# A graph kernel's relational passes: TensorE turns tile i-1 first, sums tile i, makes the first sums of tile i+1, and transforms tile i-1 last

## The chip, the cores and the metric

The kernel runs on one core of one Trainium2 chip. The metric is the device time of one execution in microseconds (us); lower is better. Ahead of the change three runs gave a median of 5129.6 us, from 5125.4 to 5138.4.

## What is computed

There are 6250 nodes with 256 features and 106,250 edges sorted by destination, each with one of 8 types. Two layers are computed: a relational one of three inner passes, and one of attention.

```python
h = relu(layernorm(x))
for l in range(3):                        # the relational layer
    xr  = einsum('nd,rde->rne', h, W_rel[l])              # 8 tables of every node
    agg = segment_sum(xr[edge_type, src], dst)            # a row of a table per edge
    h   = relu(agg + h @ W_root[l] + bias[l])
x = x + h
h = relu(layernorm(x)) @ Wv + bv          # the attention layer
attn = softmax over the edges of each destination of leaky_relu(q[src] + k[dst])
out = x + segment_sum(h[src] * attn, dst)
```

## The kernel before

All is float32. The nodes stand in NT = 49 tiles of 128, the edges that are no self-loops in 787 chunks of up to 128, and four chunks are a group (197 groups). The self-loop of a node needs no gather: its row of the table is on the chip when the tile is transformed.

The program has five stages: the first transform of every tile (to about 377 us), pass 0, pass 1 and pass 2 of the relational layer (`l` = 0, 1, 2), and the attention. A pass begins with the table of transformed rows in DRAM (8 x 256 values per node) and does this:

- **Gathers.** GpSimd (POOL) issues one indirect DMA per chunk (L676, `gather_pass`), which fetches 128 rows of 1 KB into a slot of `ring`. The ring holds RINGS = 10 groups. For group n POOL waits until the window sums of group n - 10 are done (semaphore `quad_done`).
- **Window sums** (the first step, L1755, `sum_windows`). The destinations of a chunk lie in a window of 32 nodes, so TensorE (PE) multiplies a mask of 128 x 32 with the chunk into 32 rows of `pair_ps`, and counts `quad_done` up once per group. Two groups are a pair. ScalarE (ACT) copies each pair out of `pair_ps` (L1503, `keep_pairs`) into one of four places. `pair_ps` has two halves, so the sums of pair p wait for the copy of pair p - 2. A tile needs about two new pairs; `new_pairs` gives them in two halves, early and late.
- **Tile sum** (L1769, `sum_tile`): seven matmuls over the kept pairs into `both_sums`. In pass 0 two more ahead of them add the root term (L1766). VectorE (DVE) adds `root` and writes `z` (L1235, `sum_up`).
- **Turn and transform** (L1646 and L1661). PE transposes z into `turn_ps`, ACT applies relu and writes `xT` (L1447), and PE multiplies xT with the next weights: four banks of 512 columns, and last the root part in a fifth bank, which lies beside `turn_ps`. ACT copies three banks into `stage` (L1509), DVE the fourth (L916). DVE adds the eight self-loop terms into `root` (L941, each waits for the one before), and last the fifth bank (L926). SyncE stores the tile of the next table.

In passes 0 and 1 PE's order in step i is: early window sums of tile i, turn of tile i-1, late window sums of tile i, transform of tile i-1, tile sum of tile i. ACT's is: early pair, relu of tile i-1, late pair, banks of tile i-1. Each engine runs its instructions in the order in which they are written and waits on semaphores; no scheduler comes between. In pass 0 DVE also adds eight self-loop terms of this pass for each tile, out of rows loaded from the table (L951, `add_first_loops`). In pass 2 the small product `to_h` (L1798) stands in the place of the transform, and a normalisation on DVE and ACT lies between the tile sum and the turn.

## Time and profile before

| what | value |
|---|---|
| median of 3 runs | 5129.6 us |
| the profiled execution | 5129.3 us, its span 5127.6 us |
| busy: PE, DVE, ACT, POOL | 3293.8, 1890.7, 1236.4, 3151.2 us |
| mean granted TensorE clock | 0.774 of full speed |
| pass 0, pass 1, pass 2, first to last gather | 1148.1, 1129.7, 1122.8 us |
| between last gather and next pass's first | 55.6, 52.9, 40.4 us |
| attention, from its first gather to the end | 1200.8 us |

The three passes with what follows each of them take 3549.5 us, 69% of the span. "Gather" stands for the instruction on POOL that issues one. A matmul in float32 has two records in the trace, so the seven of a tile sum are shown as x14. A matmul's record has the start from the profiler and an end that is modelled; when its result was signalled is seen only at those who wait for it. A row of the windows view gives a stretch, its length, then for PE, its weight loads, DVE, ACT and POOL the busy time with the count of instructions, then the granted TensorE clock, the share of busy DMA engines and GB/s. A row of a timeline ends with the idle time of its engine just before and what ended it, in brackets; rows of other engines and weight loads are left out. The releaser "remote" is one that the profile could not name.

### The profile page before, as it was taken

How to read it: one execution, taken by the hardware profiler on the slowest of the kernel's cores; microseconds unless marked ns; L12 is line 12 of the kernel's file. 1: busy time of each engine (PE TensorE's matmuls, PEld its weight loads, DVE VectorE, ACT ScalarE, POOL GpSimd, SP SyncE). 2: the span in 40 equal slices, each digit the busy share in tenths (PEclk: the TensorE clock that was granted, in tenths of full speed). 3: DMA queues.
4: the chain of work that ended last, by engine and by line, in shares of the span. 5: the costliest groups of instructions: out<-in, count | busy, mean ns of one | idle time of the engine just before them, and what ended most of it. 6: DMA issues, size and time to landing. Idle time of an engine off the chain costs nothing.

```text
span 5127.6 us, 48875 instructions
## 1 busy us (share of the span) xinstructions
PE 3293.8 (64%) x14171; PEld 1990.6 (39%) x14171; DVE 1890.7 (37%) x4736; ACT 1236.4 (24%) x2949; POOL 3151.2 (61%) x3305
## 2 busy tenths in 40 slices
PE   9994777776773676777665434443344677676666
PEld 4442333333431333333332223222222555565555
DVE  4543444443542232332232122222223454544444
ACT  2220111111110111111111000000002666666665
POOL 1126666666665666666664667676764666666664
PEclk9995888878886787888787666666666878778888
DMA  6544555554653344444443333333332333333332
GB/s 210 187 183 132 190 185 191 185 186 167 204 182 129 122 144 130 141 135 139 133 142 104 99 102 106 104 103 101 106 101 77 102 103 102 101 103 102 100 100 79
DMA packets 239997, 680.99 MB, mean 133 GB/s; under 512 B 60188, under 2 KB 111988, under 8 KB 215028
## 3 DMA queue, kind: packets, MB, share of 16 engines
q0 software_dynamic: 152400, 419.03, 28.0%
q1 hardware_dynamic: 73256, 245.85, 13.0%
q10 hardware_dynamic: 14076, 12.93, 0.9%
q8 instruction: 124, 2.03, 0.2%
q14 instruction: 141, 1.16, 0.1%
HBM read 501.99 MB, written 175.58 MB: 132 GB/s over the span
## 4 chain that ended last, share of the span: by engine, by line
another core or an unknown queue 31%; PE 29%; issue 14%; POOL 12%; DVE 6%; DMA 6%; ACT 2%; DVEq 1%; POOLq 0%; ACTq 0%; SPq 0%
PE bank L1661 18%; POOL ring L676 12%; DMA ring<-h_table,code 5%; PE pair_ps L1755 4%; PE both_sums L1769 4%; DVE root L941 2%; PE turn_root L1646 1%; ACT stage L1509 1%; PE bank L1798 0%; ACT xT L1447 0%; PE turn_root L1661 0%; DVE z L1235 0%; DVEq L940 0%; DVE z L907 0%
## 5 line engine op out<-in xcount | busy, mean ns | idle before, releaser
L676 POOL DMA_INDIRECT ring<-table,code x2361 | 2327.0, 986 | 1225.8 <-issue 733.7
L1661 PE MATMUL bank<-wide,xT 128*128 128x512 f32 x2352 | 1181.9, 660 | 206.9 <-ACT xT L1447 145.9
L676 POOL DMA_INDIRECT ring<-h_table,code x787 | 747.9, 950 | 461.4 <-issue 249.8
L1661 PEld LDWEIGHTS bank<-wide,xT 128*128 128x128 f32 x2352 | 489.1, 215 | 850.6 <-issue 660.7
L1769 PE MATMUL both_sums<-masks 128*128 128x256 f32 x2058 | 550.4, 426 | 320.2 <-issue 174.7
L1503 ACT COPY masks<-pair_ps 128x512 f32<-128x512 f32 x297 | 173.2, 583 | 2143.0 <-remote 1480.6
L1769 PEld LDWEIGHTS both_sums<-masks 128*128 128x128 f32 x2058 | 445.6, 219 | 416.7 <-issue 341.6
L1866 PE MATMUL pair_ps<-ring,stage 128*128 x1764 | 519.6, 445 | 98.1 <-ACT stage L1583 97.2
L1755 PE MATMUL pair_ps<-ring,masks 128*32 128x256 f32 x4722 | 450.3, 478 | 127.5 <-DMA ring<-table,code 76.6
L1646 PE MATMUL turn_root<-ident,z 128*128 128x128 f32 x392 | 104.1, 356 | 564.3 <-DVE z L1235 247.9
L1866 PEld LDWEIGHTS pair_ps<-ring,stage 128*128 128x128 f32 x1764 | 380.9, 229 | 159.1 <-issue 104.7
L941 DVE SCALAR_TENSOR_TENSOR root<-bank,loops,root 128x256 f32<-128x256 f32 x686 | 330.7, 482 | 197.1 <-ACT stage L1509 83.9
L1373 DVE TENSOR_SCALAR masks<-masks,ring 128x128 f32<-128x128 f32 x882 | 199.1, 303 | 487.4 <-issue 273.3
L1646 PEld LDWEIGHTS turn_root<-ident,z 128*128 128x128 f32 x392 | 49.6, 166 | 663.1 <-DVE z L1235 282.0
L1816 PE MATMUL bank<-ident,masks 128*128 128x128 f32 x931 | 174.3, 317 | 188.3 <-issue 117.2
L1261 DVE TENSOR_TENSOR stage<-both_sums,root 128x256 f32<-128x256 f32 x49 | 20.8, 425 | 722.3 <-remote 416.9
L1509 ACT COPY stage<-bank 128x512 f32<-128x512 f32 x294 | 170.4, 588 | 465.8 <-PE bank L1661 346.3
L1567 ACT ACTIVATE masks<-node_row,local 128x128 f32<-128x128 f32 x931 | 281.8, 393 | 0.0
L1755 PEld LDWEIGHTS pair_ps<-ring,masks 128*32 128x32 f32 x4722 | 151.3, 126 | 331.6 <-issue 277.3
L1235 DVE TENSOR_TENSOR z<-both_sums,root 128x256 f32<-128x256 f32 x98 | 41.5, 424 | 621.3 <-remote 482.8
L1544 ACT ACTIVATE wide<-bank,low_key 128x512 f32<-128x512 f32 (+1 forms) x245 | 163.6, 668 | 413.6 <-PE bank L1816 201.3
L1822 PE MATMUL bank<-ident,wide 128*128 128x128 f32 x931 | 182.0, 328 | 98.7 <-ACT wide L1577 84.8
(247 smaller groups left out, 2841.2 us busy)
## 6 DMA issues: line engine op xcount, KB each, us to landing
table<-stage SPq DMA_DIRECT2D x144, 1024.0 KB
back<-table SPq DMA_DIRECT2D x49, 1024.0 KB
ring<-table,code POOLq DMA_INDIRECT x2361
ring<-h_table,code POOLq DMA_INDIRECT x787
h_table<-stage SPq DMA_DIRECT2D x49, 130.0 KB
back<-h_table ACTq DMA_DIRECT2D x49, 130.0 KB
features<-xT SPq DMA_DIRECT2D x49, 128.0 KB, 4.0
first_T<-features SPq DMA_DIRECT2D x49, 128.0 KB
```

Of the source, the lines that this page charges most:

```text
L676: pool.indirect_dma_start(slot(c % RING, width), None, table, bass.IndirectOffsetOnAxis(ap=code[:, c:c + 1], axis=0)).then_inc(landed[n % ...
L941: nc.vector.scalar_tensor_tensor(root[:, i, :], bank[t // 2][:, t % 2 * D:(t % 2 + 1) * D], loop_weight(i, t), root[:, i, :] if t else bia ...
L1373: last = nc.vector.tensor_scalar(masks[:, b, s, :], masks[:, b, s, :], -FAR, source, ALU.mult, ALU.add)
L1509: nc.scalar.copy(stage[:, b, 512 * q:512 * (q + 1)], bank[q][:, :]).then_inc(evacuated[q], 1)
L1567: last = nc.scalar.activation(masks[:, b, s, :], node_row[:, :], ACT.Abs, scale=-1.0, bias=local[:, bass.ds(i, 1), s])
L1646: last = nc.tensor.transpose(turn_ps[:, k, :], z[:, b, k * P:(k + 1) * P], ident[:, :])
L1661: last = nc.tensor.matmul(bank[q][:, 0:width], xT[:, b, k, :], weights[:, k, 512 * q:512 * q + width], start=(k == 0), stop=(k == K - 1))
L1755: last = nc.tensor.matmul(pair_ps[p % 2][at_row:at_row + WINDOW, q % PAIR * D:(q % PAIR + 1) * D], window_masks(k)[:, c % CHUNKS_AT_ONCE, ...
L1769: last = nc.tensor.matmul(sum_ps[b][:, 0:D], masks[:, b, s, :], quad_sums(first_quad(i) + s), start=(s == 0 and l > 0), stop=(s == SPAN - 1))
L1816: last = nc.tensor.transpose(score_ps[c % 2][:, s % GROUP * P:(s % GROUP + 1) * P], masks[:, b, s, :], ident[:, :])
L1822: last = nc.tensor.transpose(attn_ps[c % 2][:, s % GROUP * P:(s % GROUP + 1) * P], scores[b][:, s * P:(s + 1) * P], ident[:, :])
L1866: last = nc.tensor.matmul(pair_ps[b][:, 0:D], attn_slot(s), at_offset(where[0][s]) if s < SLOTS else own_rows[:, b, 0:D], start=(s == 0), ...
```

## The change

The order of the three passes is another; no arithmetic is added or removed. On PE step i becomes: turn of tile i-1, tile sum of tile i, all window sums of tile i+1, transform of tile i-1 with its root part first. The window sums of tile 0 stand ahead of the loop. PE now waits, ahead of the turn, until DVE has added the root part of the tile before. On ACT relu comes first, then the pairs of tile i+1, then the banks. On DVE the tile before is evacuated (`next_table(l, i - 1, ...)`), its root part is added first and takes over the addition of the bias, and the self-loop terms follow. POOL's code and its waits are unchanged. SyncE's code is unchanged as well.

```diff
@@ -92,9 +92,7 @@
         return max(t for t in range(NT) if first_quad(t) // PAIR <= p) + 1
 
     def new_pairs(t):
-        pairs = range(pairs_to(t - 1), pairs_to(t))
-        half = (len(pairs) + 1) // 2
-        return pairs[:half], pairs[half:]
+        return range(pairs_to(t - 1), pairs_to(t))
 
...
@@ -910,8 +908,11 @@
             def evacuate(l, i, use, b, first=False, bias_at=False):
                 q = R // 2 - 1
                 if not first:
+                    dve.wait_ge(transformed[b], CREDIT + NB * use + 1)
+                    nc.vector.tensor_tensor(root[:, i, :], bank[NB - 1][:, 0:D], bias_row[:, :], ALU.add
+                                            ).then_inc(evacuated[NB - 1], 1)
                     add_loops(l, i, use, b, range(0, R - 2))
-                dve.wait_ge(transformed[b], CREDIT + NB * use + q + 1)
+                dve.wait_ge(transformed[b], CREDIT + NB * use + (q + 1 if first else q + 2))
                 dve.wait_ge(stored[b], table_stored(l, b, use))
                 nc.vector.tensor_copy(stage[:, b, 512 * q:512 * (q + 1)], bank[q][:, :]).then_inc(evacuated[q], 1)
                 if first:
@@ -920,11 +921,6 @@
                     nc.vector.tensor_copy(root[:, i, :], bias_row[:, :]).then_inc(evacuated[NB - 1], 1)
                     return
                 add_loops(l, i, use, b, range(R - 2, R))
-                dve.wait_ge(transformed[b], CREDIT + NB * use + NB)
-                settle(dve, loops_done((l - 1) * NT + i, R))
-                dve.wait_ge(root_step, loops_done((l - 1) * NT + i, R))
-                nc.vector.tensor_tensor(root[:, i, :], bank[NB - 1][:, 0:D], root[:, i, :], ALU.add
-                                        ).then_inc(evacuated[NB - 1], 1)
 
             def loop_weight(i, t):
                 return loops[:, bass.ds(i, 1), t]
@@ -935,11 +931,13 @@
                     if t % 2 == 0 and t // 2 < R // 2 - 1:
                         settle(dve, CREDIT + l * NT + i + 1)
                         dve.wait_ge(evacuated[t // 2], CREDIT + l * NT + i + 1)
-                    if t:
+                    if t == 0:
+                        dve.wait_ge(evacuated[NB - 1], CREDIT + l * NT + i + 1)
+                    else:
                         settle(dve, loops_done((l - 1) * NT + i, t))
                         dve.wait_ge(root_step, loops_done((l - 1) * NT + i, t))
                     nc.vector.scalar_tensor_tensor(root[:, i, :], bank[t // 2][:, t % 2 * D:(t % 2 + 1) * D], loop_weight(i, t),
-                                                   root[:, i, :] if t else bias_row[:, :], ALU.mult, ALU.add
+                                                   root[:, i, :], ALU.mult, ALU.add
...
@@ -1250,7 +1250,9 @@
                     upcoming_masks(l, i + 2)
                     if l == 0 and i + 1 < NT:
                         add_first_loops(i + 1, (i + 1) // 2, 1 - b)
-                    next_table(l, i, j, b)
+                    if i:
+                        next_table(l, i - 1, (i - 1) // 2, 1 - b)
+                next_table(l, NT - 1, PAIRS, 0)
...
@@ -1516,28 +1518,28 @@
 
             for l in range(L - 1):
                 conv_head(l)
+                keep_pairs(l, new_pairs(0))
                 for i in range(NT + 1):
-                    early, late = new_pairs(i) if i < NT else ((), ())
-                    keep_pairs(l, early)
                     if i:
                         j, b = divmod(i - 1, 2)
                         use = (l + 1) * USES[b] + j
                         relu_turned(use, b, transformed[b], NB * use)
-                    keep_pairs(l, late)
+                    if i + 1 < NT:
+                        keep_pairs(l, new_pairs(i + 1))
                     if i:
                         for q in range(R // 2 - 1):
                             keep_bank(l + 1, use, b, q)
 
             conv_head(L - 1)
+            keep_pairs(L - 1, new_pairs(0))
             for i in range(NT + 1):
-                early, late = new_pairs(i) if i < NT else ((), ())
-                if i:
-                    deviation(NT + i - 1)
-                keep_pairs(L - 1, early)
                 if i:
                     j, b = divmod(i - 1, 2)
                     relu_turned(L * USES[b] + j, b, h_ready[b], j)
-                keep_pairs(L - 1, late)
+                if i < NT:
+                    deviation(NT + i)
+                if i + 1 < NT:
+                    keep_pairs(L - 1, new_pairs(i + 1))
...
@@ -1776,17 +1778,18 @@
             for l in range(L - 1):
                 far_conv(l)
                 pe.wait_ge(weights_loaded, weights_of(l + 1))
+                sum_windows(l, new_pairs(0))
                 for i in range(NT + 1):
-                    early, late = new_pairs(i) if i < NT else ((), ())
-                    sum_windows(l, early)
                     if i:
                         j, b = divmod(i - 1, 2)
+                        pe.wait_ge(evacuated[NB - 1], CREDIT + (l + 1) * NT + i - 1)
                         turn_sum(l, j, b)
-                    sum_windows(l, late)
-                    if i:
-                        transform((l + 1) * NT + i - 1, (l + 1) * USES[b] + j, b, AHEAD + REST)
                     if i < NT:
                         sum_tile(l, i, i // 2, i % 2)
+                    if i + 1 < NT:
+                        sum_windows(l, new_pairs(i + 1))
+                    if i:
+                        transform((l + 1) * NT + i - 1, (l + 1) * USES[b] + j, b, ROOT_FIRST)
...
+            sum_windows(L - 1, new_pairs(0))
             for i in range(NT + 1):
-                early, late = new_pairs(i) if i < NT else ((), ())
-                sum_windows(L - 1, early)
                 if i:
                     j, b = divmod(i - 1, 2)
                     turn(L * USES[b] + j, b)
-                sum_windows(L - 1, late)
+                if i < NT:
+                    sum_tile(L - 1, i, i // 2, i % 2)
+                if i + 1 < NT:
+                    sum_windows(L - 1, new_pairs(i + 1))
                 if i:
                     to_h(j, b)
```

On PE, in the middle of pass 1 (line numbers of each program's own text), this stands before for one step and the first row of the next:

```order
L1755 MATMUL pair_ps<-ring,masks 32x256 x8
L1646 MATMUL turn_root<-ident,z 128x128 x2
L1755 MATMUL pair_ps<-ring,masks 32x256 x8
L1661 MATMUL bank<-wide,xT 128x512 x8
L1661 MATMUL turn_root<-wide,xT 128x256 x2
L1769 MATMUL both_sums<-masks 128x256 x7
```

And this now:

```order
L1648 MATMUL turn_root<-ident,z 128x128 x2
L1771 MATMUL both_sums<-masks 128x256 x7
L1757 MATMUL pair_ps<-ring,masks 32x256 x16
L1663 MATMUL turn_root<-wide,xT 128x256 x2
L1663 MATMUL bank<-wide,xT 128x512 x8
```

The two halves of the window sums are joined and stand between the tile sum and the transform; the turn no longer stands between them.

On ACT, at the same place, one step before:

```order
L1503 COPY masks<-pair_ps 128x512
L1447 ACTIVATE xT<-turn_root 128x256
L1503 COPY masks<-pair_ps 128x512
L1509 COPY stage<-bank 128x512 x3
L1503 COPY masks<-pair_ps 128x512
```

And now, one step and the first rows of the next:

```order
L1449 ACTIVATE xT<-turn_root 128x256
L1505 COPY masks<-pair_ps 128x512 x2
L1511 COPY stage<-bank 128x512 x3
L1449 ACTIVATE xT<-turn_root 128x256
L1505 COPY masks<-pair_ps 128x512 x2
```

The relu (ACTIVATE) no longer stands behind a pair copy of its own step; the bank copies still stand behind two.

On DVE, one tile of pass 0 before:

```order
L1235 TENSOR_TENSOR z<-both_sums,root 128x256
L971 SCALAR_TENSOR_TENSOR masks<-row_node,node_row 128x896
L962 TENSOR_TENSOR masks<-rel_T,node_row 128x512
L951 SCALAR_TENSOR_TENSOR root<-back,loops,root 128x256 x8
L941 SCALAR_TENSOR_TENSOR root<-bank,loops,bias_row 128x256
L941 SCALAR_TENSOR_TENSOR root<-bank,loops,root 128x256 x5
L916 COPY stage<-bank 128x512
L941 SCALAR_TENSOR_TENSOR root<-bank,loops,root 128x256 x2
L926 TENSOR_TENSOR root<-turn_root,root 128x256
```

And now:

```order
L1235 TENSOR_TENSOR z<-both_sums,root 128x256
L969 SCALAR_TENSOR_TENSOR masks<-row_node,node_row 128x896
L960 TENSOR_TENSOR masks<-rel_T,node_row 128x512
L949 SCALAR_TENSOR_TENSOR root<-back,loops,root 128x256 x8
L912 TENSOR_TENSOR root<-turn_root,bias_row 128x256
L939 SCALAR_TENSOR_TENSOR root<-bank,loops,root 128x256 x6
L917 COPY stage<-bank 128x512
L939 SCALAR_TENSOR_TENSOR root<-bank,loops,root 128x256 x2
```

The addition of the root bank moved from the end of the tile's additions to their head, but stands behind the masks and the eight additions of `add_first_loops`. From `L912` on the rows belong to tile i-1, where before all rows belonged to tile i.

## Rows read from the trace of the kernel before

**Rows 1.** Windows of three passes and one end: stretch, its us, then by engine.

```profile
377.30:1525.40 1148.10, 799.79 (x3424) 436.91 (x3425) 513.90 (x1066) 146.54 (x274) 780.21 (x787) 0.80 0.54 182
1581.00:2710.70 1129.70, 743.21 (x3133) 380.57 (x3134) 314.25 (x588) 146.34 (x274) 769.89 (x787) 0.78 0.42 135
2710.70:2763.60 52.90, 48.40 (x206) 26.27 (x205) 25.23 (x51) 11.09 (x21) 0.00 (x0) 1.00 0.25 97
2763.60:3886.40 1122.80, 451.36 (x2411) 275.78 (x2412) 237.78 (x715) 82.58 (x184) 776.89 (x787) 0.63 0.35 103
```

**Rows 2.** What the gathers of pass 0 waited for: us, times.

```profile
  PE pair_ps L1755: 74.8, 23
  remote: 67.2, 26
```

**Rows 3.** The same for pass 1 and, last two, pass 2.

```profile
  remote: 98.6, 34
  PE pair_ps L1755: 36.5, 15
...
  remote: 95.9, 30
  PE pair_ps L1755: 22.3, 9
```

**Rows 4.** Timeline, one step in pass 1: start, us, engine, line.

```profile
2272.54 1.37 POOL L676 DMA_INDIRECT ring<-table,code  x1 [2.28 <-PE pair_ps L1755]
...
2273.33 10.09 PE L1661 MATMUL bank<-wide,xT 128*128 128x512 f32 x16 [1.85 <-ACT xT L1447]
2274.22 0.94 POOL L676 DMA_INDIRECT ring<-table,code  x1 [0.30 <-issue]
...
2284.12 3.19 PE L1769 MATMUL both_sums<-masks 128*128 128x256 f32 x14
...
2287.23 1.07 PE L1755 MATMUL pair_ps<-ring,masks 128*32 128x256 f32 x16
...
2291.36 0.44 PE L1646 MATMUL turn_root<-ident,z 128*128 128x128 f32 x2 [3.06 <-DVE z L1235]
...
2295.20 0.59 ACT L1503 COPY masks<-pair_ps 128x512 f32<-128x512 f32 x1 [12.88 <-PE pair_ps L1755]
```

**Rows 5.** Timeline of PE, then of ACT, at the start of pass 1.

```profile
1623.50 1.08 PE L1755 MATMUL pair_ps<-ring,masks 128*32 128x256 f32 x8 [3.90 <-DMA ring<-table,code]
...
1639.30 0.59 ACT L1503 COPY masks<-pair_ps 128x512 f32<-128x512 f32 x1 [33.72 <-remote]
1675.70 0.59 ACT L1503 COPY masks<-pair_ps 128x512 f32<-128x512 f32 x1 [35.81 <-remote]
```

**Rows 6.** Timeline of POOL: first gathers after three pauses.

```profile
2249.64 1.37 POOL L676 DMA_INDIRECT ring<-table,code  x1 [1.96 <-remote]
...
3311.34 0.94 POOL L676 DMA_INDIRECT ring<-table,code  x1 [4.83 <-remote]
...
2852.22 0.95 POOL L676 DMA_INDIRECT ring<-table,code  x1 [7.64 <-remote]
```

**Rows 7.** Windows from the gather after one pause to the next pause's end.

```profile
2238.00:2249.60 11.60, 7.77 (x56) 4.91 (x54) 6.38 (x13) 2.00 (x5) 7.55 (x8) 0.96 0.55 182
...
3265.50:3311.30 45.80, 18.95 (x104) 11.73 (x104) 10.48 (x33) 3.59 (x8) 31.54 (x32) 0.65 0.36 103
...
2763.60:2852.20 88.60, 8.65 (x64) 1.85 (x64) 2.67 (x3) 1.76 (x3) 61.74 (x64) 0.50 0.34 101
```

**Rows 8.** Groups by line, 400 to 1600 us: two that pass 0 alone has.

```profile
L951 DVE SCALAR_TENSOR_TENSOR root<-back,loops,root 128x256 f32<-128x256 f32 x392 | 190.8, 487 | 12.3
...
L1766 PE MATMUL both_sums<-first_root,first_T 128*128 128x256 f32 x196 | 51.3, 385 | 3.3 <-issue 3.3
```

**Rows 9.** Timeline, a step in the end of pass 1.

```profile
2740.12 7.13 PE L1661 MATMUL bank<-wide,xT 128*128 128x512 f32 x16 [0.47 <-ACT xT L1447]
...
2747.09 1.03 PE L1661 MATMUL turn_root<-wide,xT 128*128 128x256 f32 x4
```

12 lines of the change are left out of this document (6 added, 6 removed).

## Prediction

> **What bounds the kernel now.** First the windows view, by stage [rows 1]. In pass 0 and in pass 1 all 787 gathers are issued while PE is busy 799.8 and 743.2 us; in pass 2, which has no transform, PE is busy 451.4 us only. Yet the three take 1148.1, 1129.7 and 1122.8 us. The reader is to see that PE's work fell by 292 us from pass 1 to pass 2 and the pass by 7 us. So PE's throughput is not the bound, and an order that merely packs PE better is worth little while gathers run. Behind the last gather it is another matter: in the 52.9 us after pass 1 PE is busy 48.4 us [rows 1].
>
> Then POOL. One gather takes 0.94 us, with 0.30 us before it [rows 4], a pace of 1.24 us, and 787 of them 976 us. Pass 1 is 154 us above that. POOL's waits on window sums are 98.6 + 36.5 = 135.1 us in 49 pieces, those of pass 0 74.8 + 67.2 = 142.0 us in 49, those of pass 2 95.9 + 22.3 = 118.2 us in 39 [rows 2, 3]. The pauses are the difference between a pass and its floor.
>
> Then what a pause waits for. In the timeline POOL waits 2.28 us until 2272.54. The transform starts at 2273.33, the tile sum at 2284.12, the window sums at 2287.23, the turn at 2291.36, and ACT's next copy of a pair only at 2295.20, after 12.88 us without work [rows 4]. The window sums take 1.07 us, but their signal is seen 8 us after their start. The start of pass 1 shows the same with nothing else on PE: its eight groups of window sums have all started by 1623.50, and ACT can copy the third pair at 1639.30 and the fourth at 1675.70 [rows 5]. The signals of PE behind window sums come late while gathers run back to back, and in one burst when POOL pauses. I can't name the mechanism from the trace, but its price can be read off. After 8 gathers the pause is 1.96 us, after 32 it is 4.83, after 64 it is 7.64 [rows 6, 7]. A line through the first and the last is 1.15 + 0.101 x n us for n gathers; at 32 it gives 4.4. At n = 16, which is 787/49, it gives 2.8 us, and 135.1/49 is 2.76. So the part of 0.101 us per gather, 80 us in a pass, is paid however the work is cut. Only the constant goes away with fewer pauses: 1.15 - 0.30 (the idle time of a common gather) = 0.85 us each.
>
> **The change, part by part.** *What is added and removed.* Per tile the DVE addition of the root bank, the eight of the self-loops and all matmuls stay in number. One wait of PE for the root addition is new; queued behind it stand the turn, the tile sum and the window sums, and for these waits ACT. I cost it at nothing in passes 1 and 2: the addition now is the first of its tile, and PE has the rest of a transform (7.13 us in the full clock) to run over it [rows 9]. POOL's and SyncE's queues are passed by nothing.
>
> *The relu ahead of the pair copies.* Before, ACT's relu stands behind an early pair copy, so the transform starts only after a burst [rows 4]. Now xT is made before the window sums are issued. What is late next is the tile sum of i+1, which needs pairs copied after the burst. From burst to next window sums there were 14.7 us (2272.54 to 2287.23), of which the transform took 10.1 [rows 4]; and the late half stood behind the turn, at 2291.7. If the transform has run ahead of the burst, turn, tile sum and window sums follow within some 5 us (0.4 + 3.2 + copies 1.2).
>
> *What that gives POOL.* A burst of one tile's window sums lets it issue 16 gathers, 20 us. If a further tile's signals get through before these are over, the pause comes after 32 gathers. Pass 2 has just this short PE step, and 787/39 = 20 gathers per pause on average, with stretches of 32 [rows 3, 7]. The new order issues window sums earlier than pass 2 does, as they no longer stand behind a turn that waits for z. I take 28 pauses in each pass (one per 28 gathers), between 49 (nothing gained) and 12 (one per 64, the longest in the rows). Sum: (49 - 28) x 0.85 = 18 us in pass 0 and in pass 1, (39 - 28) x 0.85 = 9 us in pass 2; 45 us together.
>
> *The end of a pass.* The window sums now run one tile ahead of the transform. When the last gather has landed, one transform more is left in passes 0 and 1: 7.1 + 0.9 = 8.0 us [rows 9], 16 us in two. Against that, of a step of about 12.4 us in the end (transform 8, tile sum 3.2, turn 0.4) some 1 us was the wait for z and relu, which is now covered; over four steps that is 4 us, 8 us in two passes. The net is +8 us; bounds 0 (the transform has run ahead) and +16. In pass 2 it is one small product and I leave it out.
>
> *Pass 0's DVE.* The root addition stands behind the masks and behind eight additions of 0.49 us, 3.9 us together [rows 8]. The turn waits for it. It is hidden if POOL's 20 us are not used up, else see the rival.
>
> *The clock.* PE's granted clock is 0.80 and 0.78 in passes 0 and 1, a mix of its two levels, and 1.00 in the end of pass 1 [rows 1]. The transform takes 7.13 us at full clock [rows 9] and 10.09 us after an idle stretch [rows 4]. If it directly follows the window sums it may run faster, but a faster PE has no buyer here, as pass 2 shows. I cost it at nothing.
>
> **A rule that says otherwise.** The trace has a window sum's signal up to some 50 us late [rows 5]. The Trainium skill, page "TensorE: Matmul & The Clock Gate", section "The cost: per-tile semaphore tail", gives the time from matmul to signal for tiled matmuls as 25 + 4.7 per tile + 26.3 per increment, in ns; for four tiles and one increment that is about 70 ns, an estimate from this page. By that rule nothing but the chain of PE, ACT and DVE would hold the ring, the new order would cut that chain, and the pauses would go. This trace doesn't agree. As a mechanism of this kernel it is the last rival below.
>
> **The sum.** The profiled execution took 5129.3 us (span 5127.6), as good as the median of 5129.6. 5129.3 - 45 + 8 = 5092 us.
>
> **Rivals.**
> - *The pauses keep their number.* Signals that are dispatched after a burst still come with the next. For it: at the start of pass 1 signals issued on a free PE came 16 and 50 us late [rows 5], and pass 1 has a pause per 16 gathers like clockwork. Against it: pass 2's 39. Time: 5129 + 8 = 5137 us.
> - *Slower: the transform is held too.* If PE can't run its transform until the window sums are signalled, each step after a burst is transform, turn, tile sum and window sums in series: the 14.7 us of rows 4, the turn's 0.4 and 1.1 for the second half of the window sums, 16.2 us. That is within POOL's 20 us. In pass 0 the 3.9 us of DVE come in, if the turn waits for the root addition in full, and the two additional matmuls ahead of its tile sum; their four records of 0.385 us overlap like those of the tile sum (3.19 us for 14, so 0.23 each), 0.9 us [rows 4, 8]. That is 21.0 us, 1.0 us too long, 49 times. It decides from 3.8 us of additional delay upward. Time: 5129 + 49 + 8 = 5186 us.
> - *Long stretches.* Window sums get so far ahead that POOL pauses once per 64 gathers. 37 pauses fewer in passes 0 and 1 (31 us each), 27 in pass 2 (23 us): 5129 - 86 + 8 = 5051 us. The only stretch of that length stands at a pass's start.
> - *Signals in time, no pauses.* 142 + 135 + 118 us of waits less the 137 x 0.30 that stay: 5129 - 354 = 4775 us. Rows 5 speak against it.
>
> **How the numbers follow.** The forecast has a chance of 0.50 (5075 to 5114), unchanged pauses 0.21, slower 0.18, long stretches 0.08, no pauses 0.03. The range of 5045 to 5150 holds the first, the second and the fourth, and the beginning of the third. Three tenths of a per cent, 15 us, are about what a measurement can tell from no change. Faster: the forecast nearly whole, the long stretches and the last, 0.59. Same: the second, 0.22. Slower 0.19.
>
> **What would show it.** In the profile after: the windows of the passes near 1130, 1112 and 1114 us; POOL's waits on window sums in about 28 pieces per pass instead of 49; between a burst and the next window sums some 5 us instead of 14.7; transform rows that start right behind window sums and not behind ACT's xT; and 55 us rather than 52.9 behind pass 1's last gather. I am wrong if the pauses stay at 49, or if the time falls although their number stays: then the law of 1.15 + 0.101 n is no property of the gathers but one of the order. I am wrong the other way if POOL's pauses become longer than the line allows for their stretch, which would show a ring that PE's serial step holds.

## The result and the profile after

On one chip, with the kernels run in turn, the kernel before took 5128.19 us (median of 12, 5123.12 to 5147.35) and the changed one 5144.26 us (median of 12, 5134.15 to 5150.48). The ratio is 1.0023, interval 1.0013 to 1.0034: 16 us slower, where 37 us less than 5129 were forecast. That is inside the 0.3% within which the prediction speaks of no change, though the interval leaves out 1. The time lies in the range given, but the gain that was forecast isn't there. The profiled execution took 5149.1 us (span 5147.3), against 5129.3 before.

The windows view of the changed kernel, for passes 0, 1 and 2, each followed by the stretch between its last gather and the next first one (columns as in [rows 1]):

```profile
376.20:1526.00 1149.80, 848.47 (x3404) 463.16 (x3405) 508.73 (x1056) 146.98 (x271) 779.56 (x787) 0.82 0.54 179
1526.00:1597.80 71.80, 60.89 (x235) 34.14 (x233) 42.33 (x85) 13.05 (x24) 0.00 (x0) 0.95 0.36 134
1597.80:2731.90 1134.10, 782.82 (x3142) 402.19 (x3142) 306.52 (x578) 146.92 (x271) 766.36 (x787) 0.80 0.42 134
2731.90:2791.00 59.10, 53.51 (x196) 28.85 (x196) 30.42 (x61) 12.95 (x24) 0.00 (x0) 0.99 0.23 95
2791.00:3910.70 1119.70, 499.43 (x2452) 283.79 (x2452) 243.07 (x723) 81.95 (x185) 772.24 (x787) 0.66 0.36 103
3910.70:3944.20 33.50, 19.73 (x102) 13.82 (x102) 15.83 (x61) 11.90 (x33) 0.00 (x0) 0.81 0.12 33
```

Against [rows 1] and the table of the profile before, the passes are +1.7, +4.4 and -3.1 us, their ends +16.2, +6.2 and -6.9 us, and the attention +2.3. So the passes hardly moved and the ends cost 15.5 us. (One profile of each kernel stands behind these differences.)

The gathers' waits by releaser, in pass 0, pass 1 and pass 2 of the changed kernel (us, times; they answer to [rows 2, 3]):

```profile
  remote: 86.0, 38
  PE pair_ps L1757: 58.1, 12
...
  remote: 99.7, 42
  PE pair_ps L1757: 43.3, 12
...
  remote: 96.3, 26
  PE pair_ps L1757: 20.9, 5
```

That is 50, 54 and 31 pauses with 144.1, 143.0 and 117.2 us, where there were 49, 49 and 39 with 142.0, 135.1 and 118.2. The forecast was 28 in each. In passes 0 and 1 there is still one pause for each of the 49 tiles. Pass 2 did lose eight of its 39, and the pass got 3.1 us shorter, but its waits fell by 1.0 us only, where the prediction's law (1.15 us for each pause) takes 9.2 away. What got shorter is POOL's busy time, 772.24 us against 776.89, so the fewer pauses gave nothing that these profiles show.

The timeline shows why the number stayed. One step of pass 1 of the changed kernel:

```profile
2580.55 9.25 PE L1663 MATMUL bank<-wide,xT 128*128 128x512 f32 x16
...
2580.93 0.94 POOL L674 DMA_INDIRECT ring<-table,code  x1 [2.34 <-remote]
...
2589.85 3.19 PE L1771 MATMUL both_sums<-masks 128*128 128x256 f32 x14
...
2592.97 1.81 PE L1757 MATMUL pair_ps<-ring,masks 128*32 128x256 f32 x23
...
2602.11 2.04 PE L1757 MATMUL pair_ps<-ring,masks 128*32 128x256 f32 x3 [0.76 <-issue]
2603.52 0.42 DVE L1235 TENSOR_TENSOR z<-both_sums,root 128x256 f32<-128x256 f32 x1 [12.02 <-remote]
2603.70 0.59 ACT L1505 COPY masks<-pair_ps 128x512 f32<-128x512 f32 x1 [13.27 <-remote]
2603.85 0.95 POOL L674 DMA_INDIRECT ring<-table,code  x1 [3.19 <-remote]
...
2604.07 0.80 PE L1663 MATMUL turn_root<-wide,xT 128*128 128x256 f32 x1
```

The burst, in which the signals that had been held back are seen together while POOL stands still, is at 2580.9; the next window sums start at 2593.0, 12.0 us later, not 5. Between them stand nearly the whole transform (four banks, 9.25 us) and the tile sum (3.19 us). The transform didn't run ahead of the burst: PE's order puts it behind all window sums of the tile to come. One step on, the last of these were issued at 2602.1, and the transform starts at 2604.07, after the next burst. Nothing that the tile sum or the window sums signalled in between was seen: DVE had been idle for 12.02 us when it took up a tile sum that had started at 2589.85, and ACT for 13.27 us when it took up a pair, both while POOL stood still. In this step, then, one burst admits one tile, as before.

### The profile page after: what moved, and what is told of

It reads as the page before. It is cut to its first block, busy times and chain, and to the rows that moved or that the text cites. A ratio compares the mean times of both kernels' runs of the same rounds, so it can differ in the third digit from the quotient of the medians.

```text
span 5147.3 us, 49020 instructions
## 1 busy us (share of the span) xinstructions
PE 3435.7 (67%) x14171; PEld 2048.1 (40%) x14171; DVE 1889.3 (37%) x4736; ACT 1238.2 (24%) x2949; POOL 3144.4 (61%) x3305
## 3 DMA queue, kind: packets, MB, share of 16 engines
q14 instruction: 140, 1.15, 0.1%
## 4 chain that ended last, share of the span: by engine, by line
PE 36%; issue 21%; another core or an unknown queue 17%; POOL 12%; DMA 7%; DVE 4%; DVEq 1%; ACT 1%; SPq 0%; POOLq 0%; ACTq 0%
PE bank L1663 16%; POOL ring L674 12%; PE both_sums L1771 7%; PE pair_ps L1757 7%; DMA ring<-h_table,code 6%; PE turn_root L1663 2%; DVEq L1234 1%; PE turn_root L1648 1%; DMA back<-table 1%; DVE root L949 1%; PE both_sums L1768 1%; PE bank L1801 1%; DVE root L939 1%; DVE masks L969 0%
## 5 line engine op out<-in xcount | busy, mean ns | idle before, releaser
L1663 PE MATMUL bank<-wide,xT 128*128 128x512 f32 x2352 | 1138.0, 632 | 60.0 <-issue 56.1
L1757 PE MATMUL pair_ps<-ring,masks 128*32 128x256 f32 x4722 | 555.9, 409 | 497.4 <-issue 407.6
L1771 PE MATMUL both_sums<-masks 128*128 128x256 f32 x2058 | 588.4, 448 | 342.6 <-issue 243.6
L1663 PEld LDWEIGHTS bank<-wide,xT 128*128 128x128 f32 x2352 | 477.0, 206 | 639.3 <-issue 629.1
L1771 PEld LDWEIGHTS both_sums<-masks 128*128 128x128 f32 x2058 | 469.4, 233 | 438.6 <-issue 354.5
L1757 PEld LDWEIGHTS pair_ps<-ring,masks 128*32 128x32 f32 x4722 | 193.1, 112 | 801.5 <-issue 720.9
L939 DVE SCALAR_TENSOR_TENSOR root<-bank,loops,root 128x256 f32<-128x256 f32 x784 | 378.2, 482 | 283.7 <-ACT stage L1511 159.7
L960 DVE TENSOR_TENSOR masks<-rel_T,node_row 128x512 f32<-128x512 f32 (+1 forms) x150 | 101.5, 679 | 381.2 <-remote 341.5
L1648 PE MATMUL turn_root<-ident,z 128*128 128x128 f32 x392 | 90.2, 312 | 221.7 <-DVE root L912 114.4
L1819 PEld LDWEIGHTS bank<-ident,masks 128*128 128x128 f32 x931 | 128.3, 163 | 251.8 <-issue 238.5
```

The lines of the kernel that those rows point to most:

```text
L939: nc.vector.scalar_tensor_tensor(root[:, i, :], bank[t // 2][:, t % 2 * D:(t % 2 + 1) * D], loop_weight(i, t), root[:, i, :], ALU.mult, AL ...
L1663: last = nc.tensor.matmul(bank[q][:, 0:width], xT[:, b, k, :], weights[:, k, 512 * q:512 * q + width], start=(k == 0), stop=(k == K - 1))
L1757: last = nc.tensor.matmul(pair_ps[p % 2][at_row:at_row + WINDOW, q % PAIR * D:(q % PAIR + 1) * D], window_masks(k)[:, c % CHUNKS_AT_ONCE, ...
L1771: last = nc.tensor.matmul(sum_ps[b][:, 0:D], masks[:, b, s, :], quad_sums(first_quad(i) + s), start=(s == 0 and l > 0), stop=(s == SPAN - 1))
L1819: last = nc.tensor.transpose(score_ps[c % 2][:, s % GROUP * P:(s % GROUP + 1) * P], masks[:, b, s, :], ident[:, :])
```

## The experiments

All times below are medians beside the kernel before on the same chip. These runs were made on four chips (numbers 11, 0, 7 and 2; the number of the first result's chip isn't on record, and "the first chip" below is the one of that result). On all four the kernel before takes 4714 to 4716 us, and in the profiles POOL doesn't pause in the passes at all, unless an edit makes it wait. So they can't show the pauses; they show the rest in the clear, which is the word for it below.

"End 0" is the stretch from pass 0's last gather to pass 1's first, "end 1" and "end 2" are those after the next two passes.

The theory: the new order has no hold on the pauses, since the transform still stands behind the window sums' waits, and the loss is made behind the last gathers, by one transform more and by SyncE's store ahead of the load. The rivals: the order does bring window sums earlier, and something else eats the gain; or the loss comes from the pauses.

**1. SyncE stores one tile later.** The changed kernel with

```diff
-                    elif i > 1:
-                        store_next(l + 1, i - 2, b)
+                    elif i > 2:
+                        store_next(l + 1, i - 3, 1 - b)
                 if l < L - 1:
+                    store_next(l + 1, NT - 3, 0)
                     store_next(l + 1, NT - 2, 1)
```

> The changed kernel, but in passes 0 and 1 SyncE issues the store of tile i-3 where it issued that of tile i-2, so that the loads for tile i+1 no longer stand behind a store whose data come one step later than before. Theory A (the end of pass 0 grew by 16 us, of which 8 to 9 us are one transform more and the rest is DVE waiting 1.5 to 2.4 us per step for rows loaded behind that store): the stretch from pass 0's last gather to pass 1's first falls from 71.8 to some 63 us, the passes themselves stay at 1150, 1134, 1120 us, total some 5136 us. Rival B (the load is late for its own length, not for the queue): 5144 us, stretch 72 us.

Measured: 4728.18 us against 4716.25, ratio 1.0024 (1.0015 to 1.0033). The expected times were written for the first chip and are some 400 us off in this run and the next three; only differences count. End 0 is 48.1 us, and 12 us of the loss are still there. What the store takes from it is seen beside run 5.

**2. Transform ahead of the window sums.** The changed kernel with both orders turned round in passes 0 and 1, on PE (below) and likewise ACT's bank copies ahead of its pair copies:

```diff
-                    if i + 1 < NT:
-                        sum_windows(l, new_pairs(i + 1))
                     if i:
                         transform((l + 1) * NT + i - 1, (l + 1) * USES[b] + j, b, ROOT_FIRST)
+                    if i + 1 < NT:
+                        sum_windows(l, new_pairs(i + 1))
```

> The changed kernel, but in passes 0 and 1 the transform of tile i-1 stands ahead of the window sums of tile i+1 on PE, and the bank copies ahead of the pair copies on ACT. Theory A (the number of POOL's pauses and their length don't depend on PE's order, and the end of a pass pays for the transform that lags by one tile more): passes within 6 us of 1150, 1134 and 1120 us, the two ends fall by 8 us each to some 60 and 52 us with four transforms behind the last gather, total some 5125 us. Rival B (the transform was run in the shade of the window sums and now delays them by 8 us per step): pauses get longer, passes 0 and 1 above 1160 us, total above 5170 us.

Measured: 4716.85 us against 4716.25, ratio 1.0003 (0.9994 to 1.0012): no loss. The rival's slower passes aren't there either: 1011.4, 1006.4 and 1006.5 us.

**3. The new order in pass 2 alone.** The kernel before, with PE's and ACT's order of the change in pass 2 only:

```diff
-                sum_windows(L - 1, early)
...
-                sum_windows(L - 1, late)
-                if i:
-                    to_h(j, b)
                 if i < NT:
                     sum_tile(L - 1, i, i // 2, i % 2)
+                if i + 1 < NT:
+                    sum_windows(L - 1, all_pairs(i + 1))
+                if i:
+                    to_h(j, b)
```

> The kernel before, with the new order in pass 2 alone. Theory A (the parts add up: pass 2 gained 3 us and its end 7 us, everything lost lies in passes 0 and 1): 5118 us, pass 2 at 1120 and its end at 33.5 us. Rival B (the differences of pass 2 are those between two executions): 5128 us.

Measured: 4717.19 us against 4716.25, ratio 0.9999 (0.9990 to 1.0008). Pass 2's part of the change does nothing to the time that can be measured here. Its windows serve as those of the old order in passes 0 and 1; the three ends:

```profile
1389.60:1433.00 43.40, 36.23 (x114) 19.57 (x114) 20.86 (x43) 7.00 (x13) 0.00 (x1) 0.91 0.21 84
2438.90:2475.80 36.90, 32.41 (x98) 17.16 (x96) 16.75 (x35) 6.42 (x12) 0.04 (x1) 0.96 0.23 90
3482.30:3508.30 26.00, 14.55 (x56) 10.23 (x54) 11.06 (x45) 9.24 (x27) 0.04 (x2) 0.76 0.11 33
```

**4. Window sums that don't read the ring.** The kernel before; the window sums still wait for the landing but read the weights' tile, so that the sums hold other numbers:

```diff
-window_masks(k)[:, c % CHUNKS_AT_ONCE, :], slot(c % RING, D),
+window_masks(k)[:, c % CHUNKS_AT_ONCE, :], wide[:, 0:D],
```

> The kernel before, with window sums that multiply a fixed piece of the weights in SBUF with the masks, not the rows gathered into the ring; all waits and signals stay (so the sums are of other numbers). Theory C (TensorE's reading of the ring, into which transfers write, is what makes the window sums come late): the sums come at once, POOL pauses seldom, each pass falls towards 1010 to 1060 us, total 4790 to 4950 us. Rival D (it is not the place that is read: waits, signals or the gathers' own backlog): pauses as before, 5128 us.

Measured: 4715.18 us against 4716.25, ratio 0.9996 (0.9987 to 1.0005). It was to tell the cause of the pauses, and there were none; it says only that reading the ring costs nothing measurable here.

**5. The changed kernel again.** Unchanged.

> The changed kernel, unchanged, timed once more beside the kernel before. On the chip of the first result it took 5144.3 us against 5128.2, and POOL paused about 50 times in passes 0 and 1 in both kernels. On the chip of the four runs so far POOL does not pause in the passes at all and the kernel before takes 4716.3 us. Theory: the loss is made behind the last gathers and has nothing to do with the pauses, so it stays in us whatever the pace is: the ends of passes 0, 1 and 2 take 16 and 6 us more and 7 us less, in sum 10 to 16 us slower (4726 to 4732 us where the kernel before takes 4716), with end 0 at 58 to 62 us against 43. The kernel that differs from this one only in that SyncE stores tile i-3 lost 12 us with an end 0 of 48.0, so if the loss were in SyncE's order alone this kernel would lose 12 + 10. Rival: the loss comes from the pauses or from the slower pace; then this kernel is within 0.1 per cent of the kernel before wherever there are no pauses.

Measured: 4731.24 us against 4715.26, ratio 1.0038 (1.0024 to 1.0051): 16 us slower, as on the first chip, with no pause in its profile. Its windows, as above:

```profile
377.40:1394.10 1016.70, 763.23 (x3502) 441.38 (x3502) 523.65 (x1080) 153.29 (x278) 777.17 (x787) 0.86 0.62 205
1394.10:1446.10 52.00, 44.46 (x136) 23.95 (x136) 29.99 (x61) 9.13 (x17) 0.00 (x0) 0.93 0.33 130
1446.10:2451.20 1005.10, 722.54 (x3220) 386.76 (x3221) 315.63 (x594) 153.96 (x279) 765.66 (x787) 0.81 0.48 153
2451.20:2495.30 44.10, 39.68 (x120) 21.32 (x118) 22.05 (x45) 8.54 (x16) 0.04 (x2) 0.96 0.25 99
2495.30:3500.90 1005.60, 475.22 (x2500) 280.16 (x2501) 247.48 (x739) 88.71 (x191) 766.19 (x787) 0.66 0.40 115
3500.90:3526.90 26.00, 14.59 (x56) 10.27 (x54) 11.06 (x45) 9.22 (x27) 0.04 (x2) 0.76 0.12 33
```

Passes 1 and 2 go at POOL's pace, 787 gathers in 1005 us, with PE busy 722.5 us in one and 475.2 in the other. The ends are 52.0, 44.1 and 26.0 against 43.4, 36.9 and 26.0 in run 3: 8.6 + 7.2 = 15.8 us, about the loss of 16.0. This sum is good to a few us only: end 2 takes 24.6 us with the old order, as in run 9's second kernel; end 0 with the old order lies between 39.5 and 43.4 us in the profiles of runs 3, 4 and 9; and the execution profiled here took 4737.8 us, 6.6 above its median.

Much of the spread of end 0 lies ahead of PE's work, in the landings of the last gathers. From the last window sums that wait for a landing (1395.98 here) to pass 1's first gather (1446.12) there are 50.1 us; with the old order the same stretch is 41.1 us in run 3, 40.7 in run 4 and 40.7 in run 9's second kernel. The later store of run 1 has 48.8 us, run 2 has 41.0. So in pass 0's end, too, the transform is worth about 8 us; what the store costs beside it is looked at below.

The chain that ended last shows the transforms. In run 3, pass 1's end, from the last landing (only the landing and the four banks of each transform are shown):

```profile
2434.24 2.79 DMA ring<-table,code
...
2438.25 8.77 PE bank L1664 x16
...
2452.33 7.13 PE bank L1664 x16
...
2464.78 7.15 PE bank L1664 x16
```

And in run 5:

```profile
2446.53 2.76 DMA ring<-table,code
...
2452.52 7.44 PE bank L1663 x16
...
2464.82 6.87 PE bank L1663 x16
...
2475.80 6.87 PE bank L1663 x16
...
2484.49 6.88 PE bank L1663 x16
```

Three transforms stand behind the last landing in the old order, four in the new. In the full clock the four banks of one take 6.9 to 7.2 us and its root part about 1 us more; the difference of the ends is 7.2. In run 2 the chain through pass 0's end has three transforms again.

Where the store comes in, the timeline of run 5 shows in pass 0's end, on SyncE, DVE and PE:

```profile
1408.39 0.32 SPq L836 DMA_DIRECT2D table<-stage  x1
...
1409.23 0.91 SPq L825 DMA_DIRECT2D back<-table  x1
...
1416.48 4.13 DVE L949 SCALAR_TENSOR_TENSOR root<-back,loops,root 128x256 f32<-128x256 f32 x8 [4.34 <-DMA back<-table]
...
1421.12 0.44 PE L1648 MATMUL turn_root<-ident,z 128*128 128x128 f32 x2 [0.95 <-DVE root L912]
```

SyncE's store waits for an evacuation that the change put one step later, and the load of the next tile's self-loop rows stands behind it in SyncE's queue. DVE waits 4.34 us for the load, and PE's turn waits 0.95 us for DVE's root addition. PE has no such wait in run 1's end 0, where the store is issued later, and waits 0.33 us in run 9's third kernel, which has the store as here. So in the clear the store's place costs 1 us of the loss or less. The medians of runs 1 and 5 (12 and 16 us of loss, on two chips, with intervals that overlap) can't tell more.

**6. Both edits together.** The edits of runs 1 and 2.

> Changed kernel with two edits in passes 0 and 1: PE's transform of tile i-1 stands ahead of the window sums of tile i+1 (and ACT's bank copies ahead of its pair copies), and SyncE stores tile i-3 instead of i-2. The first edit alone gave 4716.9 us and an end 0 of 42.2, the second alone 4728.2 and 48.0, the kernel before 4716.3. Theory (the loss is one transform more behind the last gather, and the store that keeps the loads of tile i+1 waiting): with both edits the end of pass 0 is no longer than with the first alone, 42 us or less, and the time 4711 to 4718 us where the kernel before takes 4716. Rival (a later store makes the end longer, as the next pass cannot begin before the last store has landed): end 0 of 46 us or more, and 4720 us.

Measured: 4715.77 us against 4715.26, ratio 1.0001 (0.9992 to 1.0010); ends of 41.6 and 39.3 us in passes 0 and 1. (The execution profiled took 4739.7 us, 24 above the median; the time is in its pass 0, not in the ends.) With the transform ahead again, the store's place is worth nothing measurable.

**7. Half the bytes.** The kernel before; the gathers of passes 0 to 2 fetch 512 bytes a row, and the window sums read that half twice, so that the output is other:

```diff
-                gather_pass(l, tables[l], D)
+                gather_pass(l, tables[l].rearrange("n (h d) -> (n h) d", h=2), D // 2)
```

> Kernel before, but each gather of passes 0 to 2 fetches 512 bytes per row instead of 1024, and the window sums read this half twice; the output is other. It keeps the number of gathers, of descriptors and of waits and halves the bytes. On a chip where POOL pauses: if the pauses come from the bytes that land, they shorten from 0.101 us per gather to about half, 40 us less per pass and 120 us in all; if they come from the gathers' count (descriptors or issuing), the passes stay within 5 us of the kernel before. On a chip without pauses: a pass of 787 gathers stays at POOL's pace, 1005 to 1015 us, and the time within 10 us of the kernel before, if the pace is that of issuing; it would fall towards 800 us only if bytes set it.

> Kernel before with gathers of 512 bytes per row instead of 1024 in passes 0 to 2, window sums read the half twice (the output is other), once more. On a chip without pauses: 4708 us as in the first run, passes of 1005 to 1011 us. On a chip with pauses it tells their cause: if they come from bytes that land, the pauses shorten by half in their part per gather, 120 us less in all (5010 us); if they come from the number of gathers or of descriptors, which is unchanged, the time stays within 15 us of 5128.

Measured in single runs: 4708.29 us against 4715.26, and 4714.45 against 4713.87 on another chip. The passes take 1011.0, 1004.6 and 1005.3 us in the first of them: with half the bytes POOL's pace is the same. On the pauses it says nothing.

**8. Run 2 again.** Unchanged.

> The kernel with PE's transform of tile i-1 ahead of the window sums of tile i+1 (and ACT's bank copies ahead of its pair copies) in passes 0 and 1, unchanged, once more. If POOL pauses in the passes on this chip (kernel before near 5128 us, some 49, 49 and 39 pauses): theory (the pauses come from gathers that run back to back and from nothing in the order of PE, ACT or DVE) expects 45 to 55 pauses in passes 0 and 1, passes of 1125 to 1155 us, ends of 50 to 56 us and a time within 0.2 per cent of the kernel before; the prediction's idea (a transform that is ahead of the burst makes a pause rarer) expects 28 pauses, 1110 to 1130 us per pass and 5080 to 5100 us. If there are no pauses on this chip: 4716 us, within 0.1 per cent of the kernel before, by both.

Measured: 4714.68 us against 4716.00, ratio 0.9994 (0.9985 to 1.0004). The ends of passes 0 and 1 are 39.0 and 39.4 us, 78.4 together (81.6 in run 2), where the changed kernel has 96.1 and the old order between 76.4 (run 4) and 80.3 (run 3).

**9. Landing waits: added in the passes, taken from the attention.** In the attention POOL waits ahead of every second group until the group before has landed. The first kernel is the one before with this in the passes too:

```diff
-                    if l == L and n and n % 2 == 0:
+                    if n and n % 2 == 0:
                         pool.wait_ge(landed[(n - 1) % RINGS], 16 * gathers_to(l, n - 1))
```

> Kernel before with the landing waits of the attention added in passes 0 to 2 as well: ahead of every second group POOL waits until the group before has landed, so that no more than 8 gathers are under way. Theory (the price of a wait is fixed at 2.05 us, as in the attention, and nothing piles up behind it): 98 waits cost 172 us in a pass, each pass takes 1170 to 1185 us. On a chip without pauses that is 490 us more in all, 5200 us; on a chip with pauses the pauses on window sums vanish (signals of PE get through at each wait) and the passes take 22, 45 and 55 us more than 1148, 1130 and 1123, 5250 us. Rival (pauses on window sums are of PE's making): on a chip with pauses both add up, and a pass takes more than 1250 us.

The second is the kernel before without both lines, in the attention too:

> Kernel before without the landing waits of POOL in the attention (98 of them, each about 2.05 us where a common gather has 0.30 us before it). Theory (where signals come in time, a landing wait is a pause that POOL pays for nothing, 1.75 us each): on a chip without pauses in the passes the attention's gathers take 787 x 1.25 = 985 to 1030 us instead of 1178 and the time falls by 150 to 170 us to about 4555, unless another engine becomes the bound; on a chip with pauses the attention takes the law of the passes, 1120 to 1150 us, and the time falls by 30 to 55 us. Rival (the attention is bound by ACT, DVE and PE, each busy 550 to 800 us of 1180 with chains between them): gathers run ahead until the ring is full, POOL waits for released slots instead, and the time falls by less than 40 us on either chip.

The third is the changed kernel without them:

> The changed kernel without the 98 landing waits of the attention. The kernel before without them took 4541.2 us where the kernel before took 4716.0. Theory (the two edits lie in different stages and both act on a chip without pauses): 4541 + 16 = 4557 us where the kernel before takes 4716. Rival (a lag that the change brings into the passes is made up for in the attention, or the gain of the freed attention is partly of its start): 4541 to 4548 us. On a chip with pauses (kernel before near 5128 us) both expect that the gathers of the attention pause on released slots like those of the passes on window sums: its 787 gathers take 1120 to 1150 us instead of 1178, the time is 5144 - 45 = 5100 us.

Measured: 5219.23 us with the waits everywhere (one run), against 4716.00; the passes take 1191, 1176 and 1170 us instead of some 1006 to 1014. (The expectation's band of 1170 to 1185 missed pass 0.) Without any, 4541.17 against 4716.00, ratio 0.9632 (0.9615 to 0.9648). The changed kernel without any, 4558.74 against 4713.87, ratio 0.9670 (0.9650 to 0.9691): its 16 us stay (4541 + 16 = 4557). The gathers of the attention with the waits (run 5) and without:

```profile
3526.90:4705.00 1178.10, 797.18 (x3625) 646.87 (x3626) 555.04 (x1689) 702.47 (x1872) 747.35 (x787) 0.79 0.37 100
```

```profile
3505.00:4504.10 999.10, 751.02 (x3603) 631.01 (x3604) 561.41 (x1688) 690.81 (x1865) 747.96 (x787) 0.83 0.44 118
```

98 waits less, 179 us less, 1.8 us each: on these chips a landing wait is paid in full, and the rival of an attention bound by ACT, DVE and PE is out. The kernel before without them is the fastest of all that ran. Whether it is so on a chip with pauses wasn't tried.

**10. A short lead, so that POOL must wait on any chip.** The three orders (before, changed, and run 2's), each with

```diff
-                    if n >= RINGS and l < L:
-                        pool.wait_ge(quad_done, l * GROUPS + n - RINGS + 1)
+                    if n >= 3 and l < L:
+                        pool.wait_ge(quad_done, l * GROUPS + n - 3 + 1)
```

> Kernel before, but in passes 0 to 2 POOL waits for the window sums of the group 3 back instead of 10 back: 12 gathers, 15 us, may be ahead of the window sums instead of 40. So PE's order binds POOL even on a chip where signals come in time. PE has a stretch of transform and tile sum of 8.9 + 3.2 = 12 us without window sums, and a group of four gathers must land first (some 3 us): theory expects short waits on window sums about once per tile, 49 per pass of 1 to 5 us, passes 0 and 1 at 1060 to 1200 us and pass 2, with its short step, at 1006 to 1040 us. It is the base for the two that follow.

> The changed kernel with the same short lead of 3 groups. Theory (the change doesn't bring window sums earlier: the transform is issued behind all window sums of the next tile, as one stretch of transform, turn and tile sum of about 12 us, as before): passes 0 and 1 within 15 us of those of the kernel before with the short lead, or longer, since window sums now stand behind a tile sum that needs the pair copies. The prediction's idea (turn, tile sum and window sums follow a burst within 5 us because the transform is done by then): passes 0 and 1 at least 20 us shorter each than those of the kernel before with the short lead.

> The changed kernel with the transform of tile i-1 ahead of the window sums of tile i+1 in passes 0 and 1 (bank copies ahead of pair copies), with the same short lead of 3 groups. Stretch without window sums: turn, tile sum, transform (which waits for the relu of this step, about 1 us), 13 us in one piece. Theory: passes 0 and 1 as long as with the changed order or up to 30 us longer. The prediction's idea, applied to the order that really has the transform ahead of the window sums: 20 us shorter than both.

Measured, one run each: 4903.42, 4929.68 and 4985.57 us. Pass 0 takes 1141, 1138 and 1211 us, pass 1 1061, 1081 and 1079, pass 2 1008, 1007 and 1006. POOL's waits on window sums in pass 1, in the three kernels in turn:

```profile
  PE pair_ps L1755: 69.5, 46
```

```profile
  PE pair_ps L1757: 90.1, 46
```

```profile
  PE pair_ps L1757: 88.0, 46
```

46 waits in all three, about one per tile, and none in pass 2, whose step has no transform. The timelines say why the new order isn't earlier. The old order, from the last window sums of a step to the next, and POOL's wait:

```profile
2044.34 1.08 PE L1755 MATMUL pair_ps<-ring,masks 128*32 128x256 f32 x8 [4.52 <-DMA ring<-table,code]
...
2058.69 1.07 PE L1755 MATMUL pair_ps<-ring,masks 128*32 128x256 f32 x16
...
2059.63 1.41 POOL L676 DMA_INDIRECT ring<-table,code  x1 [2.28 <-PE pair_ps L1755]
2059.83 0.59 ACT L1503 COPY masks<-pair_ps 128x512 f32<-128x512 f32 x1 [6.05 <-PE pair_ps L1755]
```

The changed order:

```profile
2031.46 1.08 PE L1757 MATMUL pair_ps<-ring,masks 128*32 128x256 f32 x8 [4.48 <-DMA ring<-table,code]
...
2046.18 1.07 PE L1757 MATMUL pair_ps<-ring,masks 128*32 128x256 f32 x16
...
2047.13 1.41 POOL L674 DMA_INDIRECT ring<-table,code  x1 [2.59 <-PE pair_ps L1757]
```

14.4 us from window sums to window sums in the old order, 14.7 in the new. What the wait for POOL's slots sees is the transform and the tile sum in one piece, in the new order with the turn between them. For a ring this short, where signals come in time, the prediction's idea (passes 20 us shorter) is refuted: pass 0 is 3.6 us shorter with the changed order, pass 1 20.3 us longer. The two ends are again longer, 46.9 and 45.1 us against 39.8 and 36.2. The expectation for run 2's order missed in pass 0, which is 70 us longer than the others, not up to 30; that wasn't followed further. An order with the transform truly ahead never ran where POOL pauses, so whether it would make pauses rarer there stays open.

## Why the prediction was wrong, step by step

- **"If the transform has run ahead of the burst, turn, tile sum and window sums follow within some 5 us."** This step failed. 12.0 us were measured on the first chip, against 14.7 before. The transform is written behind window sums that wait for landings, so it starts only behind them: 9.25 us of it still stood between the burst and the tile sum, where the prediction had taken them out. The order listing in the section on the change shows it; I had read "xT is made earlier" as "the transform runs earlier".
- **"I take 28 pauses in each pass."** This step failed in passes 0 and 1: 50 and 54. For these two passes the first rival, unchanged number, was the case (chance 0.21), and its 5137 us is 7 us below the result. That the result lies in the range given owes nothing to the forecast's mechanism. The rows of the step above bear a simple reading: each step of PE needs a signal (z, a copied pair) that is seen only when POOL stands still, so one burst admits one tile. That is argued from the timeline of the first chip, not tested. In pass 2, 39 fell to 31, a part of what was forecast there; the pass fell by 3.1 us, not 9, and not by its waits. Its end fell by 6.9 us, which no term of the sum has.
- **The law 1.15 + 0.101 n.** With 50 pauses for 787 gathers, n is 15.7 and the law gives 2.7 us a pause; measured 144.1/50 = 2.88 in pass 0. In pass 1 n is 14.6, the law 2.6, measured 143.0/54 = 2.65. In pass 2 n is 25.4, the law 3.7, measured 117.2/31 = 3.78. So it fits the length of a pause within 0.15 us in the first result. The gain that the prediction drew from it isn't borne out: pass 2, the only one with fewer pauses, has 1.0 us less of waits for eight pauses less, not 9.2. Errors of 0.1 us per pause are enough to hide such a gain. Nor is the law a property of gathers as such: on the four chips of the experiments there is no pause at all at the same pace, and at pass 1's end the last landing is seen 2.8 us after its issue. What makes the difference stays open. POOL's floor of 976 us, from 0.94 us a gather, was low as well: some gathers take longer, and in the clear a pass takes 1005 us.
- **The end of a pass: "the net is +8 us".** Mis-sized. The one transform more is right: 8.0 us taken, 6.9 to 7.2 and 1 measured. The covered waits, which should give 4 us back per pass, give about 1: net 7.2 us in pass 1 in the clear, 6.2 on the first chip. In pass 0 the end grew by 16.2 us on the first chip, and by about 9 in the clear, counted from the last landing. The ends' sum over the three passes on the first chip is 15.5 us, where 8 stood in the sum; the rest of pass 0's is in the next point.
- **"POOL's and SyncE's queues are passed by nothing."** Failed for SyncE. Its code is unchanged, but its store waits for an evacuation that moved by a step, and the load behind it came late. In the clear that costs 1 us of PE's time or less (runs 1, 5 and 9). In pass 0's end of the changed kernel on the first chip it costs more. There PE's turn waits three times for DVE's root addition, 1.52, 2.26 and 2.40 us, 6.2 us in all; in the old order's end PE has no wait for it. With one transform more (8 us) that is most of the 16.2. Two of the three:

```profile
1543.02 0.93 SPq L825 DMA_DIRECT2D back<-table  x1
...
1549.67 4.13 DVE L949 SCALAR_TENSOR_TENSOR root<-back,loops,root 128x256 f32<-128x256 f32 x8 [5.10 <-DMA back<-table]
1554.31 0.69 PE L1648 MATMUL turn_root<-ident,z 128*128 128x128 f32 x2 [2.26 <-DVE root L912]
...
1566.47 4.13 DVE L949 SCALAR_TENSOR_TENSOR root<-back,loops,root 128x256 f32<-128x256 f32 x8 [5.78 <-DMA back<-table]
...
1571.12 0.62 PE L1648 MATMUL turn_root<-ident,z 128*128 128x128 f32 x2 [2.40 <-DVE root L912]
```

  Run 1, which takes this wait away, was made in the clear only, so what it would give on the first chip isn't shown.

- **"Pass 2's end: I leave it out."** It fell by 6.9 us on the first chip (one profile of each), and in the clear it grew by 1.4 us (26.0 against 24.6). Why they differ stays open.
- **PE isn't the bound while gathers run, and its clock is worth nothing.** Right: the mean clock rose from 0.774 to 0.793 with no gain, and in run 5 the passes 1 and 2 take 1005.1 and 1005.6 us with PE busy 722.5 and 475.2.
- **The slower rival** (serial step, 5186 us) had its sign right and its place wrong: the passes gained no delay beyond 4.4 us; the loss is behind them. The wait that it named for pass 0, the turn behind DVE's eight additions and the root addition, is real, and it costs in that pass's end, where no gather of POOL hides it.
- **The rule on a matmul's signal.** On the first chip it didn't fit (signals up to some 50 us late). In the clear run 10's first trace has the window sums of 2058.69 end at 2059.76 (a modelled end) and ACT's copy start at 2059.83, 0.07 us. The Trainium skill, page "TensorE: Matmul & The Clock Gate", section "The cost: per-tile semaphore tail", gives 25 + 4.7 per tile + 26.3 per increment, in ns; for four tiles and one increment that is about 70 ns, an estimate from this page. There the trace agrees. So what the last rival describes exists, in the clear: 4716 us for the old order, where 4775 was worked out, and 4731 for the new. It isn't of the new order's making.

## What to carry to other kernels

To bring a step forward in an engine's order is worth nothing if a wait for landings still stands ahead of it: read where the moved work now stands, not where its operand is made. In this kernel POOL set the pace, and the order of the other engines cost only where POOL was silent; count what stands behind the last transfer, here one transform more in each of two passes, 7 to 8 us each. And an unchanged queue is passed when what it waits for moves: follow its first wait, and what is queued behind that.

## What the runs showed of the hardware

- The same kernel takes 5128 us in the first measurement and 4714 to 4716 us on four chips later (4709 to 4727 over all their runs). Most of it is POOL's pauses: passes of 1148, 1130 and 1123 us against 1013, 1005 and 1006 (run 9's second kernel, whose passes are those of the kernel before). The ends are 56, 53 and 40 against 42, 37 and 25: with the pauses PE is a tile further behind when the last gather is issued, and pass 1's end has four transforms (from 2714.42, 2727.74, 2740.12 and 2752.56 in the chain of the kernel before), not three. The attention, whose gathers have landing waits, takes about as long on all (1201 us on the first chip, 1209 in run 5). Whether it is the chip or its condition at the time can't be told from one chip with pauses.
- A landing wait ahead of every 8 gathers costs 1.8 us each where signals come in time. Without them the kernel takes 4541.2 us, 3.7% less than before. From the first chip alone, whose passes without such waits take 1123 to 1148 us, I had estimated 30 to 55 us for a chip with pauses; no run shows that.
- POOL's pace of 1.25 us per gather of 128 rows is the same for rows of 512 and of 1024 bytes (passes 1 of 1004.6 and 1005.4 us).
